# A linear attention stage: the output projection as three bf16 passes on a split activation, and another order of stages

## What is computed

```python
xn = layer_norm(x, norm_g, norm_b)
q = (xn @ Wq + bq).reshape(B, T, H, dh)
k = (xn @ Wk + bk).reshape(B, T, H, dh)
v = (xn @ Wv + bv).reshape(B, T, H, dh)
q = jax.nn.softmax(q, axis=-1)
k = jax.nn.softmax(k, axis=1)
ctx = jnp.einsum('bnhd,bnhl->bhdl', k, v)
y = jnp.einsum('bnhd,bhdl->bnhl', q, ctx).reshape(B, T, D)
emb_out = jax.nn.silu(emb) @ emb_W + emb_b
scale, shift = jnp.split(emb_out, 2, axis=-1)
h = layer_norm(y, sn_g, sn_b) * (1.0 + scale) + shift
h = jax.nn.silu(h) @ out_W + out_b
return x + gate_msa * h
```

## Time and profile before

| what | value |
|---|---|
| median of 3 runs | 1266.47 us (1264.91 to 1266.75) |
| the profiled execution's own time | 1262.96 us |
| its span | 1261.2 us |
| granted TensorE clock, mean | 0.973 of full |
| PE / DVE / ACT / POOL busy | 89% / 76% / 63% / 67% |
| linear stage, first rstd to end of span | 876.1 to 1261.2 us |

### The profile page before, as it was taken

How to read it: one execution, slowest core, us unless ns; L and a number is a source line. 1 busy time by engine, 2 the same in 40 slices (tenths; PEclk the granted TensorE clock), 3 DMA queues, 4 the chain that set the end, 5 groups by cost and what they waited for, 6 DMA issues and landing times. The chain is left out here.

```text
span 1261.2 us, 37486 instructions
## 1 busy us (share of the span) xinstructions
PE 1128.5 (89%) x11946; PEld 818.5 (65%) x12098; DVE 960.6 (76%) x2338; ACT 795.3 (63%) x2141; POOL 848.9 (67%) x1018
## 2 busy tenths in 40 slices
...
DMA packets 138945, 68.13 MB, mean 54 GB/s; under 512 B 76544, under 2 KB 137600, under 8 KB 138880
## 3 DMA queue, kind: packets, MB, share of 16 engines
...
## 5 line engine op out<-in xcount | busy, mean ns | idle before, releaser
L1128 PE MATMUL f_ps_y<-w_fc,f_h_split 128*128 128x256 bf16 x1536 | 172.7, 273 | 1.4 <-DVE f_branch L1247 1.4
L1155 PE MATMUL f_ps_h<-f_x_split,w_fc 128*128 128x512 bf16 x737 | 166.4, 383 | 4.3 <-DVE f_biases L1278 1.4
L1128 PEld LDWEIGHTS f_ps_y<-w_fc,f_h_split 128*128 128x128 bf16 x1536 | 150.2, 98 | 22.5 <-issue 1.7
L657 POOL TENSOR_TENSOR e_split<-e_full,e_split 128x1024 bf16<-128x1024 f32 x64 | 136.5, 2133 | 39.7 <-ACT e_full L730 39.7
L1255 DVE TENSOR_TENSOR f_h_split<-f_h,f_h_split 128x512 bf16<-128x512 f32 x64 | 64.0, 1002 | 104.3 <-ACT f_h L1114 104.2
L1489 ACT ACTIVATE l_z_t<-l_ps_yt,shift,scale 128x64 f32<-128x64 f32 x256 | 82.6, 402 | 92.3 <-PE l_ps_yt L1555 56.2
L1155 PEld LDWEIGHTS f_ps_h<-f_x_split,w_fc 128*128 128x128 bf16 x768 | 75.6, 99 | 88.7 <-issue 3.3
L1113 ACT ACTIVATE f_h_split<-f_ps_h,columns 128x512 bf16<-128x512 f32 x128 | 89.1, 696 | 66.5 <-POOL f_h_split L1074 36.2
L790 PE MATMUL ps_s<-qk_t,k_pairs 128*128 128x64 bf16 x3072 | 102.6, 195 | 29.0 <-DMA k_pairs<-qk_t 25.4
L790 PEld LDWEIGHTS ps_s<-qk_t,k_pairs 128*128 128x128 bf16 x3072 | 97.9, 99 | 37.3 <-issue 19.0
L1074 POOL TENSOR_TENSOR f_h_split<-f_h,f_h_split 128x512 bf16<-128x512 f32 x64 | 79.7, 1255 | 36.6 <-ACT f_h L1114 36.6
...
## 6 DMA issues: line engine op xcount, KB each, us to landing
v_pairs<-v_split SPq DMA_DIRECT2D x128, 66.0 KB, 2.1
k_pairs<-qk_t SPq DMA_DIRECT2D x256, 32.0 KB, 2.2
...
l_gate<-in_cond ACTq DMA_DIRECT2D x128, 64.0 KB, 2.6
...
```

The lines of the kernel that those rows point to most:

```text
L657: pool.tensor_tensor(flat(e_split[a][:, LO]), flat(e_full[:]), flat(e_split[a][:, HI]), ALU.subtract).then_inc(e_lo_made, 1)
L1128: last = pe.matmul(ps_y[:, i], h_split[a][:, hs, f, i * P:(i + 1) * P], m.w_fc2[:, ws, f], start=(f == 0 and k == 0), stop=(f == F_CHUNKS ...
L1155: last = pe.matmul(ps_h[f % 4][:], m.w_fc1[:, ws, c, f * P:(f + 1) * P], x2_split[a][:, xs, c], start=(k == 0 and c == 0), stop=(k == 2 an ...
```

## The change

In the linear stage the activation silu is split like the other operands: ACT's new `silu_high` rounds it to bf16, POOL's new `silu_low` subtracts that from the fp32 value, and `project` (now lag 12) runs three bf16 passes against a `m.w_out3` that is split as well, 6 matmuls of 256 columns. The weight's split is made in the feed-forward pass, on ACT and DVE, from `out3_full`. The lists of stages stand in another order with some other lags. The wait of DVE on y's statistics, in the loop, moves from `v_low` to `q_lower`; `q_copy` waits on `kq_turned` itself. In setup several semaphores are united, with the counts that this needs; the PE's wait for the widened v bias (`laid_out`, 2) now covers the copy of cond_t as well.

```diff
-        self.w_out3 = sb("w_out3", [P, NC_, C], F32)
+        self.w_out3 = sb("w_out3", [P, 2, NC_, C], BF16)
...
-            pe.wait_ge(v_bias_widened, 1)
+            pe.wait_ge(laid_out, 2)
...
-            sp.dma_start(m.w_out3[:], out_w.rearrange(CHUNKED, p=P)).then_inc(m.linear_here, 16)
+            sp.dma_start(out3_full[:], out_w.rearrange(CHUNKED, p=P)).then_inc(out3_here, 16)
...
-            sp.wait_ge(m.linear_here, 16)
+            sp.wait_ge(qvk3_here, 16 * 10)
...
+                    act.wait_ge(out3_here, 16)
+                    act.activation(m.w_out3[:, HI], out3_full[:], ACT.Copy).then_inc(out3_hi_made, 1)
...
+                    dve.wait_ge(out3_hi_made, 1)
+                    dve.tensor_tensor(m.w_out3[:, LO], out3_full[:], m.w_out3[:, HI], ALU.subtract)
...
-                reuse(pool, out_done, t, 2)
+                reuse(pool, silu_lo_made, t, 2)
...
+            def silu_low(t):
+                a = t.slot(2)
+                pool.wait_ge(silu_hi_made, t.n + 1)
+                reuse(pool, out_done, t, 2)
+                pool.tensor_tensor(silu_split[a][:, LO], silu[a][:], silu_split[a][:, HI], ALU.subtract
+                                   ).then_inc(silu_lo_made, 1)
...
-            pipeline(pool, [(5, softmax), (10, silus), (8, last_inverse_deviations), (-1, inverse_deviations),
-                            (12, add)])
+            pipeline(pool, [(5, softmax), (10, silus), (-1, inverse_deviations), (14, add), (11, silu_low),
+                            (8, last_inverse_deviations)])
...
+            def silu_high(t):
+                a = t.slot(2)
+                act.wait_ge(silu_made, t.n + 1)
+                reuse(act, out_done, t, 2)
+                act.activation(silu_split[a][:, HI], silu[a][:], ACT.Copy).then_inc(silu_hi_made, 1)
...
-            pipeline(act, [(3, v_high), (9, load_gate), (9, modulate), (1, x3_high), (3, k_exponentials),
-                           (3, q_exponentials), (5, k_high), (5, q_copy), (9, tanhs), (13, store)])
+            pipeline(act, [(3, v_high), (10, load_gate), (9, modulate), (3, k_exponentials), (5, k_high),
+                           (9, tanhs), (1, x3_high), (5, q_copy), (16, store), (3, q_exponentials),
+                           (10, silu_high)])
...
-                for c in range(NC_):
-                    last = pe.matmul(ps_out[:], silu[a][:, c], m.w_out3[:, c], start=False, stop=(c == NC_ - 1))
+                for i, (zs, ws) in enumerate(SPLITS):
+                    for c in range(NC_):
+                        last = pe.matmul(ps_out[:], silu_split[a][:, zs, c], m.w_out3[:, ws, c],
+                                         start=False, stop=(i == 2 and c == NC_ - 1))
...
-            pipeline(pe, [(5, turn_kq), (6, k_v_first), (11, project), (6, k_v_second), (2, qkv), (7, q_kv),
-                          (0, turn_x), (8, turn_y)])
+            pipeline(pe, [(6, k_v_first), (5, turn_kq), (6, k_v_second), (12, project), (2, qkv), (7, q_kv),
+                          (8, turn_y), (0, turn_x)])
...
-            pipeline(dve, [(-2, statistics), (3, q_maxima), (3, k_maxima), (8, y_statistics), (3, q_lower),
-                           (3, v_low), (-1, aggregate), (8, y_aggregate), (4, total), (1, x3_low), (8, y_hats),
-                           (-1, hat), (11, residual), (5, k_low), (6, mask)])
+            pipeline(dve, [(3, q_maxima), (3, k_maxima), (8, y_statistics), (3, q_lower), (8, y_aggregate),
+                           (-2, statistics), (-1, aggregate), (3, v_low), (4, total), (6, mask), (8, y_hats),
+                           (12, residual), (1, x3_low), (5, k_low), (-1, hat)])
```

94 lines of the change are left out of this document (47 added, 47 removed).

## The result

The changed kernel takes 1274.91 us at the median of six runs (1271.78 to 1277.42); the kernel before, on the same chip, 1264.73 (1262.35 to 1266.75). The ratio is 1.0077, with a 95% interval of 1.0057 to 1.0097: slower by about 10 us, where 4 us less was forecast. (The forecast of 1262.5 us started from 1266.5, the median of three runs of the kernel before; the six here give 1.7 us less.) The profiled execution of the changed kernel took 1275.55 us, its span is 1273.7 us, 12.5 us more than the span before.

What follows compares the result with a forecast made beforehand. TensorE was taken to bound the linear loop at 5.65 us per tile; loop -7.2, front -2.0, drain +5.2 and setup 0 summed to -4.0 us from 1266.5, giving 1262.5 us, range 1257 to 1271.5.

Steps and rivals of the forecast that it cites:

- TensorE's step, 5.65 to 5.50: Linear loop: bf16 projection saves TensorE 0.14 to 0.15 us per tile, -7.2 us over 48 tiles.
- Rival C: Loop and drain: cheaper TensorE transitions and a drain not GpSimd's alone, -8 us, 1258.5 us; chance 0.13.
- Does anyone else take its place: Loop at 5.50 us: no, VectorE needs 5.3 us and GpSimd 5.2, so TensorE stays the bound.
- rival A: Loop: x_hat waits for GpSimd's softmax, VectorE's step 5.7 us, no loop gain, +5.6 us, 1272 us; chance 0.19.
- any wait that VectorE has left stands ahead of q_maxima: Loop, VectorE: argument against x_hat meeting softmax, as no wait was expected between aggregate and hat.
- GpSimd and ScalarE in the loop: Loop: silu_low brings GpSimd to 5.2 us; silu_high's 0.3 us fits ScalarE's 1.40 us idle time.
- Rival D: Loop: ScalarE becomes the bound as DMA issue adds to its work, +3.7 us, 1270 us; chance 0.08.
- Rival B: Loop: x_hat collides only in some tiles, period near 5.56 us, -0.6 us in all, 1266 us; chance 0.15.
- The front: First tiles of the linear stage: VectorE's lost wait and TensorE's gain give -2 us (0 to -4).
- The drain: Behind the last loop tile: GpSimd's added silu_low and a longer last chain cost +5.2 us (+3.5 to +6.5).
- the one behind y_hat 63, +2.5: End of the drain: last tile's extra ScalarE copy, GpSimd subtraction and queueing, less a shorter projection, +2.5 us.
- the weight's split: Feed-forward pass: splitting w_out3 once on ScalarE and VectorE costs 0 (to +1) us.

Runs made afterwards that it cites:

- e2: Changed kernel with hat moved ahead of x3_low and k_low in VectorE's list: 1260.89 us, ratio 0.9972 to the kernel before.
- e3: Changed kernel with all four engines' stage orders and the y_stats wait as in the kernel before, leaving the bf16 projection's part: 1265.03 us, ratio 1.0007.
- e4: Kernel before, fp32 projection kept, with the changed kernel's stage orders: 1266.83 us, ratio 1.0020.
- e1: Changed kernel with hat moved ahead of k_low only in VectorE's list: 1263.40 us, ratio 0.9998 to the kernel before.
- e7: Changed kernel with idle matmuls added on TensorE in the drain, ahead of its waits: 1274.16 us, ratio 1.0066 to the kernel before.
- e6: e2 with silu_low done by VectorE instead of GpSimd for tiles 53 to 63: 1260.01 us, ratio 0.9959 to the kernel before.
- e9: e6 with the adds of tiles 54 to 63 on VectorE too, other adds at lag 13: 1259.79 us, ratio 0.9958 to the kernel before.
- e11: e9 with idle TensorE matmuls in the drain and the last group's output stored tile by tile: 1257.97 us, ratio 0.9942 to the kernel before.
- e8: Kernel before with only the change's united setup semaphores: 1264.05 us, ratio 0.9996.

## Why the prediction was wrong, point by point

- **TensorE's step, 5.65 to 5.50: right.** Where nothing else was in the way the steps are 5.48 us (e2), and without the new order 5.50 (e3). So the gain of 0.15 us per tile is the projection's. The order gives nothing: with the fp32 projection it costs TensorE 0.04 us (e4, 5.69 against 5.65), with the bf16 one the two orders differ by 0.02, and in the old one some waits are left. Rival C, which needs a gain of 0.2 us per tile, stays short of it even here. The six matmuls hold 0.65 us to the next start; 0.66 was the count.
- **"Does anyone else take its place": here it failed, on VectorE.** I had its instructions at 5.3 us and x_hat at 0.4 in them, so that TensorE would set the step at 5.50. Measured are 5.78 us for VectorE's step with x_hat at 0.84, and TensorE waits for it in every tile. The mechanism stood in the text as rival A, with its place and its price: step 5.7 us, 1272 us. It came to 5.77 us, as the mean of 45 tiles, and 1274.9 us. What failed is the weight of it, 0.19, and the condition: "if x_hat comes later than that half". By my sum x_hat was to start 0.05 us ahead of softmax's q half; it did start 0.06 us ahead (1058.24 and 1058.31), and lost. The e2 rows show that even 0.11 us was not enough there and 0.16 was; over all traces the change lies between 0.09 and 0.13 us. In the kernel before x_hat started 0.17 us ahead of softmax's k half (1054.01 and 1054.18), just enough, and that half's 0.71 us against 0.62 for the q half in the earlier trace rows was the price that the other side paid. The earlier trace rows had the case that decides, a start at 908.35 against 908.39, 0.04 us ahead, and 0.81 us long. I read it as a coincidence of starts and not as a bound: ahead by 0.04 loses. With that reading A is the likeliest case, and 0.19 was far too little for it.
- **"Against it: any wait that VectorE has left stands ahead of q_maxima": right, and no argument.** Nothing between aggregate and hat varies, so the collision is the same in every tile instead of never.
- The Trainium skill, "SBUF — State Buffer", § Who interferes with whom, gives the exclusion of a VectorE instruction in a two-port mode and a GpSimd one. By that rule, the traces agree: x_hat ends 0.15 us behind the GpSimd operation in the changed kernel and in e1. "Issue order, not op shape, decides who blocks", it says; measured at the rows' starts the order is seen with an offset of 0.09 to 0.13 us against VectorE. That x_hat runs in such a mode is taken from its behaviour; no row here names the mode.
- **GpSimd and ScalarE in the loop: right.** GpSimd waits some 0.8 us before each rstd; ScalarE waits before z_t:

```profile
1058.97 1.29 ACT L1499 ACTIVATE l_z_t<-l_ps_yt,shift,scale 128x64 f32<-128x64 f32 x4 [1.30 <-PE l_ps_yt L1574]
```

  Rival D is out: the gate's DMA issue takes nothing from it.
- **Rival B** asked for collisions in some tiles and a period of 5.56. e2 has them in one tile of four, and the period stays TensorE's 5.48: the slack of the other three takes it up. e4, with collisions in three of four, has 5.70, which is TensorE's own time as well.
- **The front: -2.7 against -2.0, right**; by e3 and e4 (68.8 and 68.7 us against 69.6) the projection and the order give about 1 us each.
- **The drain: right in kind, +7.6 against +5.2.** From y_hat 58 to 63 it is 21.0 us against the 20.6 of the sum; of these 0.7 are the low stretch of the clock that e2 and e7 don't have (20.3 and 20.2). The stretch ahead of it was to gain 0.3 and lost 0.3. The term that was mis-sized is the one behind y_hat 63, +2.5, measured +3.9 (10.5 to 14.4): I had followed the last tile's own chain. What stands there is a row of projections through one ps_out, four of them where the kernel before had three, since the lag went from 11 to 12, and GpSimd's queue beside it, about equally long. The lower clock of the last projections is a part of it: with three of the four at 0.82 us e2 takes 14.1. What it would be with all four, and no matmuls in the way, no run shows. In e6 GpSimd's late adds held the row of projections; e9 and e11, which take these off too, come to 13.6 and 11.8.
- **Setup: 0, right (e8), and the weight's split is within its bound.** From the first to the last record of the feed-forward stage's second product (f_ps_y) it is 335.0 us against 334.7 before. The ten traces that have the split all show 335.0, the three that don't (before, e4, e8) 334.7: a real cost of 0.35 us.
- **Ahead of the linear stage the trace of after has +2.9 us, and 2.4 of them are not from the change.** They stand ahead of the feed-forward stage, whose first product starts at 512.06 against 509.61. e1 and e6, whose program is the changed kernel's up to there, start it at 509.45 and 509.51, as the kernel before does. The execution of after has a granted clock of 0.72 between 50 and 56 us, in the attention stage, where before, e1 and e6 have 1.00. The other 0.4 us are the weight's split, nearly all.
